# Four pipeline stages, earlier loads and a second buffer for the feed-forward part of a fused attention and feed-forward kernel

## The reference

```python
x = L0_attn_x                                    # (8, 1024, 128)
x = x + layernorm(attention(layernorm(x), Wq, Wk, Wv, Wb, Wa, A_log, dt_bias, Wo, conv_q, conv_k, conv_v))
x = x + layernorm(ffn(layernorm(x), W_r, W_k, W_v, mu_r, mu_k))
return x

def ffn(x, W_r, W_k, W_v, mu_r, mu_k):
    x_prev = concatenate([zeros((B, 1, C)), x[:, :-1, :]], axis=1)
    xr = mu_r * x + (1.0 - mu_r) * x_prev
    xk = mu_k * x + (1.0 - mu_k) * x_prev
    r = sigmoid(einsum('btc,dc->btd', xr, W_r))
    k = einsum('btc,dc->btd', xk, W_k)
    return r * einsum('btc,dc->btd', square(relu(k)), W_v)
```

## Time and profile before

| | us |
|---|---|
| median of three runs | 3398.29 (3397.6 to 3399.78) |
| the profiled execution | 3398.14 |
| its span in the trace | 3396.3 |
| start of the feed-forward part in the trace | 3199.9 |

### The profile page before, as it was taken

How to read it: one execution, slowest core, us unless ns; L and a number is a source line. 1 busy time by engine, 2 the same in 40 slices (tenths; PEclk the granted TensorE clock), 3 DMA queues, 4 the chain that set the end, 5 groups by cost and what they waited for, 6 DMA issues and landing times. The chain is left out here.

```text
span 3396.3 us, 200052 instructions
## 1 busy us (share of the span) xinstructions
PE 2822.9 (83%) x80034; PEld 2335.4 (69%) x80034; DVE 2551.4 (75%) x5466; ACT 2654.5 (78%) x5678; POOL 2053.6 (60%) x3430
## 2 busy tenths in 40 slices
PE   6588888888888888888888888888888888888565
PEld 5477777777777777777777777777777777777443
DVE  6577778777777878787777878777787877777353
ACT  2588888888888888888888888888888888888453
POOL 1366666666666666666666666666666666666245
PEclk9699999999999999999999999999999999999787
DMA  2233333333333333333333333333333333333211
GB/s 65 67 80 79 79 84 80 82 77 81 80 78 81 81 83 78 81 77 80 80 79 83 80 83 77 81 80 78 81 82 83 78 81 80 79 80 80 47 44 38
DMA packets 931827, 260.24 MB, mean 77 GB/s; under 512 B 824256, under 2 KB 898240, under 8 KB 931776
## 3 DMA queue, kind: packets, MB, share of 16 engines
q1 hardware_dynamic: 931616, 259.01, 34.1%
q0 software_dynamic: 160, 0.53, 0.0%
HBM read 203.29 MB, written 56.11 MB: 76 GB/s over the span
## 5 line engine op out<-in xcount | busy, mean ns | idle before, releaser
L853 DVE SCALAR_TENSOR_TENSOR cv<-ps,w_v,cv 128x512 f32<-128x512 f32 x768 | 576.7, 751 | 401.7 <-ACT cv L720 383.6
L853 DVE SCALAR_TENSOR_TENSOR cv<-ps,w_kq,cv 128x512 f32<-128x512 f32 x768 | 575.4, 749 | 96.3 <-ACT cv L720 73.0
L511 PE MATMUL ps<-xnT,w_kq 128*128 (+1 forms) x1024 | 300.0, 414 | 111.9 <-DVE cv L853 94.6
L511 PE MATMUL ps<-xnT,w_v 128*128 (+1 forms) x1024 | 297.1, 411 | 82.0 <-DVE cv L853 69.3
L978 POOL TENSOR_TENSOR sc<-tabP,sc 128x8 f32<-128x8 f32 x128 | 26.1, 204 | 491.4 <-DVE sc L868 491.4
L511 PEld LDWEIGHTS ps<-xnT,w_kq 128*128 128x128 f32 x1024 | 173.9, 190 | 190.6 <-issue 169.7
L1013 POOL TENSOR_TENSOR Sg<-S,tabR 128x512 f32<-128x512 f32 x256 | 262.0, 1044 | 65.9 <-DVE S L961 65.9
L1022 POOL TENSOR_TENSOR accT<-accT,X 128x512 f32 (+1 forms) x128 | 163.7, 1279 | 220.1 <-ACT Y L818 220.1
L818 ACT ACTIVATE X<-ps,sc 128x128 f32<-128x128 f32 x512 | 145.9, 368 | 180.8 <-PE ps L707 180.8
L953 DVE SCALAR_TENSOR_TENSOR Rr<-ps,sc,Vt 128x128 f32<-128x128 f32 x1024 | 275.3, 342 | 0.8 <-ACT Vt L766 0.8
L766 ACT ACTIVATE Vt<-ps,sc 128x128 f32<-128x128 f32 x1024 | 272.2, 365 | 0.7 <-PE ps L571 0.7
(11 more groups left out here) (201 smaller groups left out, 7928.7 us busy)
## 6 DMA issues: line engine op xcount, KB each, us to landing
Lm<-scrD SPq DMA_DIRECT2D x256, 128.0 KB, 3.0
scrN<-Nd SPq DMA_DIRECT2D x256, 128.0 KB, 2.6
ex<-scrG SPq DMA_DIRECT2D x256, 128.0 KB, 2.9
Z<-scrZ SPq DMA_DIRECT2D x256, 128.0 KB, 3.3
X<-scrX SPq DMA_DIRECT2D x512, 64.0 KB
w_kq<-wtab SPq DMA_DIRECT2D x128, 132.0 KB, 2.5
w_v<-wtab SPq DMA_DIRECT2D x128, 132.0 KB, 2.8
wo_s<-wo SPq DMA_DIRECT2D x128, 128.0 KB, 2.6
```

Source lines behind the costliest of these rows:

```text
L511: last = nc.tensor.matmul(pj[:, 4 * g:4 * g + 4, 0:CW], w[:, (j % 2) * P:(j % 2 + 1) * P], xnT3[:, 4 * g:4 * g + 4, bass.ds((n % NC) * C, ...
L853: nc.vector.scalar_tensor_tensor(cv4[:, j], pj[:, :, k:k + C], tap(j, k), cv4[:, j], ALU.mult, ALU.add).then_inc(conv[j].sem, 1)
```

## The change

The feed-forward part goes from three stages to four. PE's iteration i is now K(i), tr(i+3), R(i), T(i+1), V(i). DVE's is the multiply of row i-1 with its statistics, the statistics of x1(i+2), the reciprocal for POOL, the statistics of tokens i+3, the two other reciprocals and the factor, and last n1(i+2). ACT's is relu and square of row i, the root for POOL, the sigmoid, the eviction to hx of row i+1, the two other roots, and the eviction of tokens i+3. x1 has a fifth buffer, and rg a second one (Lm), so that the multiply of row b waits for POOL's read of row b-2. V writes to banks 6 and 7, once the sigmoid has read R there, instead of 4 and 5.

The weights wf go into tabP and the eight rows of x into xnT, whose contents are no longer needed then. SP loads all of them inside the attention part: its list is written out, and ahead of the last step's sp_wo it waits for two signals of that step, then issues the transfer of wf (192 KB) and eight transfers of x (512 KB each). The scaling of the weights on DVE moves behind the first statistics, and PE's wait for it to K(0). The last row is normalised by DVE instead of POOL. ACT loads the table for the root at the start.

The diff, cut to its core:

```diff
+                sp_body(sp, STEPS - 2, STEPS - 1, None)
+                sp.wait_ge(dmn_ok.sem, dmn_ok.at(STEPS - 1))
+                sp.dma_start(wf_s, wf).then_inc(f_w.sem, 16)
+                sp.wait_ge(proj[3].sem, proj[3].at(STEPS - 1))
+                for b in range(NB):
+                    sp.dma_start(tok(x_s[b]), x_tok[b]).then_inc(f_x[b].sem, 16)
+                sp_body(sp, STEPS - 1, None, None)
...
-        x1 = (BD["PT"], BD["NM"], BD["X0"], Rr)
+        x1 = (BD["PT"], BD["NM"], BD["X0"], Rr, Vt)
-        n1, ka, sg, rg = BD["Y"], U, S, oo
+        n1, ka, sg = BD["Y"], U, S
+        rg = (oo, Lm)
...
             @block.vector
+                for i in range(-3, NB + 1):
+                    if i >= 1:
+                        dve.wait_ge(f_v.sem, i)
+                        if i >= 3:
+                            dve.wait_ge(f_n2.sem, i - 2)
+                        nc.vector.tensor_tensor(rg[(i - 1) % 2][:], bank(6, 2), sg[:], ALU.mult).then_inc(f_rg.sem, 1)
+                        dve.wait_ge(f_rg.sem, i)
+                        stats(t3(rg[(i - 1) % 2]), 2, i - 1)
+                    if 0 <= i + 2 < NB:
+                        b = i + 2
+                        dve.wait_ge(f_r1.sem, b + 1)
+                        stats(t3(x1[b % 5]), 1)
+                    if i >= 1:
+                        dve.wait_ge(f_sd[2].sem, i)
+                        nc.vector.reciprocal(rs[2 + (i - 1) % 2], sd[2]).then_inc(f_r2.sem, 1)
...
+                    if i + 3 < NB:
+                        b = i + 3
+                        dve.wait_ge(f_tr.sem, b + 1)
+                        stats(bank(0, 2).rearrange("p (j d) -> p j d", j=NT), 0)
...
+                    if 0 <= i + 2 < NB:
+                        b = i + 2
+                        dve.wait_ge(f_r1s.sem, b + 1)
                         if b:
                             dve.wait_ge(f_t1.sem, b)
                         for j in range(NT):
-                            last = nc.vector.tensor_scalar(t3(n1)[:, j, :], t3(x1[b % 4])[:, j, :], ag[1][:, j, 0:1], rs[1][:, j:j + 1],
+                            last = nc.vector.tensor_scalar(t3(n1)[:, j, :], t3(x1[b % 5])[:, j, :], ag[1][:, j, 0:1], rs[1][:, j:j + 1],
...
             @block.tensor
-                pe.wait_ge(f_wm.sem, 1)
-                pe.wait_ge(f_zc.sem, 1)
-                for i in range(-2, NB):
+                for i in range(-3, NB):
+                    if i == 0:
+                        pe.wait_ge(f_wm.sem, 1)
+                        pe.wait_ge(f_zc.sem, 1)
...
+                        pe.wait_ge(f_ka.sem, i + 1)
+                        pe.wait_ge(f_sg.sem, i + 1)
                         for j in range(NT):
-                            last = nc.tensor.matmul(unit(ps, 16 + j), unit(ka, j), wf_s[:, 2 * P:3 * P], start=True, stop=True)
+                            last = nc.tensor.matmul(unit(ps, 24 + j), unit(ka, j), wf_s[:, 2 * P:3 * P], start=True, stop=True)
```

More of the change, by code:

```diff
@@ L1354, in pool_body @@
                 pool_elim(pool, n)
+        f_w = sig("f_w")
+        f_x = [sig("f_x%d" % b) for b in range(NB)]
+        x_s = [xnT3[:, b, HALO:HALO + T] for b in range(NB)]
+        wf_s = tabP[:, 0:3 * P]
+        tok = lambda t: t.rearrange("p (j d) -> p j d", j=NT)
         def program(eng, body):
@@ L1451, in _ @@
             def _(sp):
[L1452 to L1461, removed]
+                for b in range(NB):
+                    sp.wait_ge(f_y.sem, b + 1)
+                    sp.dma_start(out_tok[b], t3(yo[b % 2])).then_inc(f_out[b % 2].sem, 16)
                 for k in range(2):
@@ L1493, in then, with stats @@
                     dve.wait_ge(f_ch.sem, chain[0])
-                def stats(src, k):
+                def stats(src, k, b=0):
                     for j in range(NT):
@@ L1500, in stats @@
                     for j in range(NT):
-                        last = nc.vector.bn_aggr(ag[k][:, j, :], st[k][:, j, :])
+                        last = nc.vector.bn_aggr(ag[k + b % 2][:, j, :], st[k][:, j, :])
                     last.then_inc(f_st[k].sem, 1)
-                dve.wait_ge(f_w.sem, 16)
-                then(nc.vector.tensor_scalar(mu1, muc[:], -1.0, 1.0, ALU.mult, ALU.add))
-                for k in range(2):
-                    nc.vector.tensor_scalar(wm[2 * k], wf_s[:, k * P:(k + 1) * P], muc[:, k:k + 1], None, ALU.mult)
-                    last = nc.vector.tensor_scalar(wm[2 * k + 1], wf_s[:, k * P:(k + 1) * P], mu1[:, k:k + 1], None, ALU.mult)
@@ L1517, in _ @@
                         dve.wait_ge(f_tr.sem, b + 1)
                         stats(bank(0, 2).rearrange("p (j d) -> p j d", j=NT), 0)
+                    if i == -3:
+                        dve.wait_ge(f_w.sem, 16)
+                        then(nc.vector.tensor_scalar(mu1, muc[:], -1.0, 1.0, ALU.mult, ALU.add))
+                        for k in range(2):
+                            nc.vector.tensor_scalar(wm[2 * k], wf_s[:, k * P:(k + 1) * P], muc[:, k:k + 1], None, ALU.mult)
+                            last = nc.vector.tensor_scalar(wm[2 * k + 1], wf_s[:, k * P:(k + 1) * P], mu1[:, k:k + 1], None, ALU.mult)
+                        last.then_inc(f_wm.sem, 1)
@@ L1579, in _ @@
                         nc.scalar.activation(sg[:], bank(6, 2), ACT.Sigmoid).then_inc(f_sg.sem, 1)
-                        root(i, 2)
+                    if 0 <= i + 1 < NB:
+                        act.wait_ge(f_t1.sem, i + 2)
+                        if i >= 0:
+                            act.wait_ge(f_r.sem, i + 1)
+                        nc.scalar.activation(hx[:, 1:1 + T], bank(2, 2), ACT.Copy).then_inc(f_ev.sem, 1)
+                    if 0 <= i + 2 < NB:
+                        root(i + 2, 1)
@@ new lines, in _ @@
+                    if i + 3 < NB:
+                        b = i + 3
+                        root(b, 0)
+                        act.wait_ge(f_nb.sem, b + 1)
+                        if b >= 5:
+                            act.wait_ge(f_y.sem, b - 4)
+                        for j in range(NT):
+                            last = nc.scalar.activation(t3(x1[b % 5])[:, j, :], unit(ps, j), ACT.Identity,
+                                                        bias=nb[:, j:j + 1], scale=rs[0][:, j:j + 1])
+                        last.then_inc(f_n0.sem, 1)
```

141 lines of the change are left out of this document (63 added, 78 removed).

## The result

The changed kernel takes 3370.32 us (median of four, 3358.29 to 3373.74) beside 3399.03 for the kernel before (median of four): ratio 0.9908, interval 0.9882 to 0.9934. A second set of the same kernel gave 3367.37 (3358.62 to 3374.60), ratio 0.9898 (0.9873 to 0.9923). The profiled execution took 3372.32 us for a span of 3370.5, so 1.8 lie around it, as forecast.

What follows compares the result with a forecast made beforehand. A loop of waits, 20.5 us a row, was taken to bound the feed-forward part. First row at 3261.0, four periods 72.3, drain 14.1 + 12.8 + 4.4, end 4.1: span 3368.7, plus 1.8 is 3370.5, put as 3370; range 3341 to 3380.

Steps and rivals of the forecast that it cites:

- The part's start stays at 3199.9.: End of attention: loads moved into its last step delay nothing, 0 us taken, bounds 0 and +2 us.
- part 1: Loads moved into the last attention step: first feed-forward row gains 2.6 us, wo_s lands near 3190, no delay.
- The hold of DVE by POOL: Steady feed-forward rows: POOL's normalise and additions hold DVE's n1 piece by piece, about 7.7 us instead of 2.1.
- 2 x 2.1: Within n1: the final add and the next row's add on POOL each hold DVE 2.1 us.
- 3 x 0.5: Within n1: two or three remaining pieces of POOL's normalise hold DVE, counted as three at 0.5 us.
- The third loop: Steady rows: multiply, statistics, root, tables, sigmoid, evictions, factor and held n1 sum to 17.9 us, taken as 18.1.
- In some rows R starts at half clock: PE in steady rows: after idling about 4 us ahead of R; row taken as 18.1 us instead of 17.9.
- Rival 1: Feed-forward rows: no collision, n1 does not hold what POOL needs; row 13.6 us, time 3344; chance 0.25.
- Rival 2: Feed-forward rows: DVE's n1 pieces keep POOL out for 2.14 us a row; loop 15.7, time 3354; chance 0.19.
- Rival 3: Feed-forward part: PE stays at half clock, slower than before, about 3412 us; chance of slower 0.03.
- Rival 4: Last attention step: wo_s or x lands late, 2 to 5 us delay, 3375; chance 0.03, shared with other sums above 3375.
- signs of being wrong in another way: Unforeseen wait at a table load or eviction, matmuls at half clock in most rows, or attention ending after 3199.9.

Runs made afterwards that it cites:

- the pairs: Separate kernel timing DVE and POOL instructions alone and together, computing nothing of the reference; 32 DVE pieces from SBUF: 8.29 us alone, 16.47 beside four POOL additions.
- the factor in PSUM: The changed kernel with the second normalisation's factor written to PSUM and n1 reading it there as scalar_tensor_tensor; 3349.54 us, ratio 0.9853.
- the small product: The changed kernel with n1's factor in PSUM, POOL's reciprocal ahead of the second statistics, and one input of the 128 by 8 product in PSUM; 3351.36 us, ratio 0.9865.

## Why the prediction was right, step by step

**What bounds the kernel.** Right: it is a loop of waits, and the 20.5 us loop went.

**Start of the part.** The first addition comes 2.89 us earlier after the part's start (10.40 against 13.29), forecast 2.6: right in size. It was put down to the early loads, which aren't needed for it: with the loads late it is 2.90.

**"The part's start stays at 3199.9."** Wrong, the failed step of part 1. It came at 3207.1, 7.2 later. 5.1 of them lie ahead of the early loads: the last load of X, just before them, is issued at 3174.7 against 3169.7, and between the profiles of all kernels anywhere from 3169.5 to 3175.5; that part is chance, or at least has no cause in the change that the runs show. The other 2.1 lie in the last step, 32.4 us against 30.3, where the comparisons above put 2 to 5 us for the early loads. What in the last step costs them stays open. The prediction charged the traffic to wo_s alone; wo_s landed at 3194.1 (forecast 3190), and its matmuls started at 3198.9, right behind those of L698: nothing waited for it. PE's clock and the gap in L653 were not among its terms. SP's issue was mis-sized as well:

```profile
3176.03 12.08 SPq L1387 DMA_DIRECT2D xnT<-x  x8
3188.23 1.92 SPq L1081 DMA_DIRECT2D wo_s<-wo  x1
```

Eight issues at 0.5 each were taken from issues of small transfers and the two of 512 KB; eight in a row take 12.08: the first two 0.43 and 0.58, the others 1.3 to 2.4, about the pace at which the rows land (1.7 to 2.7 apart). And the rate was 290 GB/s, not 245.

**The hold of DVE by POOL.** The mechanism was right and is shown three times (the pairs, the factor in PSUM, the small product). "2 x 2.1" for the additions was right: 2.05 each in the pairs. Two terms were off. "3 x 0.5" for L1491's pieces: they cost nothing here (six pieces of n1 start 0.26 apart, as before), and 0.53 in 8.3 us in the pairs. And there is no wait ahead of the factor in this kernel (0.5). So n1 takes 5.9 to 6.2 in four rows (4.2 in the fifth, where it meets one addition), not 7.7. From the one pair in the earlier trace rows a hold by POOL's one-input pieces could not be told from one by its two-input additions; the prediction took the larger.

**The third loop.** 17.2 us on the mean against 17.9, taken as 18.1. It held 1.7 us less in n1 and 0.5 less ahead of it, and more in R: behind the multiply R takes 5.3 to 6.3 us at half clock in most rows, where the statistics, root and table (4.0) were to be the longer way (R at full clock takes 3.84). "In some rows R starts at half clock" is the term that was too small, 0.2 a row for 1.5 to 2.5. PE's wait ahead of R, forecast at about 4, was 2.1 to 2.6, and 5.0 in one row.

**Drain and end.** 13.45 + 13.10 + 4.31 = 30.9 against 31.3; the end 4.1 as forecast.

**Sum.** From the part's start, first output row 59.8 (forecast 61.1), four periods 68.7 (72.3), drain 30.9 (31.3), end 4.1: 163.4 (rounded terms) against 168.8. The part was 5.4 us faster and began 7.2 later than forecast: 3370.5 against 3368.7. That the time was met so closely is luck: two errors of opposite sign nearly cancel, and the median of 3370 lies between the two groups of the changed kernel's times. What was right by its reasoning is the way and the rough size: the old loop gone, a collision of DVE and POOL in its place, and the price of an addition.

**The rivals.** Rival 1 (no collision, 3344) did not come, but is what the kernel turns into with the factor in PSUM: 3349.5 with the late start of the part, 3346.9 without the early loads. Rival 2: POOL's eight pieces take 6.2 to 6.4, so POOL isn't kept out. Rival 3: half clock in most R, but the mean clock of the part rose from 0.74 to 0.80. Rival 4: a later end of attention did come, by another way than wo_s. Of the prediction's own signs of being wrong in another way two came: R at half clock in most rows, and an end of attention later than 3199.9.

**The rule of the shared ports.** By the Trainium skill, in SBUF — State Buffer, § Who interferes with whom, GpSimd holds a VectorE instruction that is in its two-port mode or reads SBUF twice for the whole of its own. For the additions, the small product with two SBUF inputs, and the freedom of what reads PSUM, the traces agree (2.05 a time; 2.18 against 0.16; 10.30 against 10.30). For POOL's tensor_scalar with one SBUF input they differ: 8.29 became 8.82, and the measurement decides.

**The table load.** By the Trainium skill, in ScalarE: Activation LUTs, § What ACT_TABLE_LOAD costs, a switch adds a drain of 1.38 us. The load in the chain above (3260.73) starts 0.01 after the eviction before it, takes 1.28, and the root follows 0.02 behind it: no drain is seen, and the measurement decides.

## What to carry to other kernels

Deeper stages put work of two engines side by side that was apart before: for each GpSimd addition with both inputs in SBUF look up which VectorE instructions can meet it. Those that were held here are a tensor_scalar from SBUF to SBUF and a product with two SBUF inputs; with one operand in PSUM (the first one as a scalar_tensor_tensor) both ran free. Do that before reordering anything: here a new order moved the collision to the next small instruction. A wait of 2 to 3 us of TensorE can have a second price in half clock behind it (1.5 to 2.5 us a row here), and one loop can run in two ways that differ by it. A load moved earlier can lengthen the stage that it moves into, even where nothing there waits for it (2.6 to 5.2 us here, the cause open), and it has to bring something that a late one doesn't. And in a loop of only eight rows the drain is worth a look of its own: it gave as much as the loop.

## What was not expected of the hardware

- An addition on GpSimd (128 x 1024, both inputs in SBUF) holds even a 128 x 8 VectorE product with two SBUF inputs until it ends: 2.18 us for 0.17; with one of the inputs in PSUM 0.16.
- GpSimd's tensor_scalar pieces hardly hold VectorE's: 32 pieces 8.82 for 8.29. Wide VectorE pieces (128 x 1024) do hold GpSimd's: 14.36 for 12.47.
- Eight issues of 512 KB in a row on SP take 11.4 to 13.2 us (10.9 in the kernel of pairs), and what stands behind them on SP goes out only then.
- TensorE's gap inside L653 of the last attention step was 1.20 to 1.27 us in three profiles without transfers of x in that step, and 1.15 to 3.74 in ten with them.
